# Attention inside a five-stage kernel: two score blocks in one PSUM bank, one reciprocal for four rows, Pool normalising every block, three copies for four, and q and k turned in the projections' banks

## What is computed

```python
x = x + quantised(layernorm(x)) @ quantised(ctx).T      # fp8 grid, blocks of 128
hidden = layernorm(x)
h = rmsnorm(hidden, attn_norm_w)
q, k, v = h @ q_w.T, h @ k_w.T, h @ v_w.T               # 16 heads of q, 4 of k and v, 128 columns each
q, k = rope(rmsnorm(q, q_norm_w)), rope(rmsnorm(k, k_norm_w))
scores = (q @ k.T) / sqrt(128)                          # causal
attn = softmax(scores) @ v                              # four q heads share one k and v head
hidden = hidden + attn @ o_w.T
moe = top-2 of 8 experts(rmsnorm(hidden, ffn_norm_w))
out = x + hidden + moe
```

## Time and profile before

| | |
|---|---|
| median of 3 runs | 1451.8 us (1449.87 to 1459.89) |
| the profiled execution | 1459.93 us, span of its instructions 1458.1 us |
| mean granted TensorE clock | 0.954 of full |
| first head's scores to the last head's values | 91 us to 1095 us, sixteen iterations |
| before it | the first sample's front and first projections |
| after it | last output projection, routing, experts (`moe`) |

### The profile page before, as it was taken

The page is one execution under the profiler, slowest core; times in us unless marked ns, Lnnn a source line. Parts: engine busy times, 40 slices in busy tenths (PEclk is TensorE's granted clock), DMA queues, the critical chain, the costliest instruction groups (busy, mean ns, idle before and its releaser), DMA issues. The chain is left out here.

```text
span 1458.1 us, 22564 instructions
## 1 busy us (share of the span) xinstructions
PE 1273.2 (87%) x6845; PEld 1025.1 (70%) x6845; DVE 837.7 (57%) x2459; ACT 719.7 (49%) x2289; POOL 382.8 (26%) x545
## 2 busy tenths in 40 slices
PE   1867899999999989789999999989994679999995
PEld 1555677787776778677767777778764569888995
DVE  7668877666876666568767666565535223222331
ACT  6447755556675655466655655556532123222331
POOL 0213222232322223032213133322210123333332
PEclk9988999999999999999999999999997689999998
DMA  2270425350535465547535565754214786774443
GB/s 95 82 265 22 147 110 176 131 196 9 221 100 205 147 217 194 180 134 209 182 134 192 178 208 177 211 193 158 87 59 174 273 290 188 206 222 79 82 74 44
DMA packets 89445, 227.85 MB, mean 156 GB/s; under 512 B 12081, under 2 KB 49841, under 8 KB 79089
## 3 DMA queue, kind: packets, MB, share of 16 engines
q1 hardware_dynamic: 75552, 201.21, 39.4%
q0 software_dynamic: 10848, 24.71, 9.3%
q10 hardware_dynamic: 2928, 0.49, 0.2%
HBM read 146.65 MB, written 79.72 MB: 155 GB/s over the span
## 5 line engine op out<-in xcount | busy, mean ns | idle before, releaser
L527 POOL TENSOR_TENSOR prob<-prob,rtotal 128x128 f32<-128x128 f32 (+2 forms) x192 | 116.7, 613 | 457.1 <-DVE rtotal L1270 430.6
L1264 DVE TENSOR_SCALAR_CACHE_REDUCE prob<-bank,nscale 128x128 f32<-128x128 f32 (+3 forms) x256 | 134.9, 544 | 164.9 <-PE bank L705 164.5
L944 ACT ACTIVATE prob<-prob,bias 128x128 f32<-128x128 f32 (+3 forms) x256 | 144.8, 566 | 153.1 <-DVE prob L1264 152.2
L669 PE MATMUL bank<-w_hi,hT_hi 128*128 128x512 f32 x480 | 175.3, 365 | 16.6 <-DVE rot L1229 16.6
L724 PE MATMUL bank<-pT,v 128*128 128x512 f32 (+3 forms) x512 | 175.8, 445 | 8.8 <-ACT pT L950 8.1
L950 ACT ACTIVATE pT<-bank 128x512 f32<-128x512 f32 (+3 forms) x256 | 103.8, 433 | 138.3 <-PE bank L713 137.9
L669 PE MATMUL bank<-w_hi,hT_lo 128*128 128x512 f32 x480 | 163.6, 341 | 0.0
L669 PE MATMUL bank<-w_lo,hT_hi 128*128 128x512 f32 x480 | 163.6, 341 | 0.0
L1529 PE MATMUL gu<-we,xT_hi 128*128 x624 | 155.9, 333 | 3.2 <-DVE xT_lo L1645 1.7
L504 POOL TENSOR_TENSOR r<-r,rot 128x640 f32<-128x640 f32 x60 | 100.2, 1670 | 189.8 <-DVE rot L1229 189.8
L703 PE MATMUL bank<-kT_hi,qT_hi 128*128 128x128 f32 (+3 forms) x256 | 103.5, 404 | 14.6 <-DVE prob L1264 14.5
(11 more groups left out here) (291 smaller groups left out, 2859.7 us busy)
## 6 DMA issues: line engine op xcount, KB each, us to landing
w_hi<-ws_scratch SPq DMA_DIRECT2D x24, 1024.0 KB, 5.2
w_lo<-ws_scratch SPq DMA_DIRECT2D x24, 1024.0 KB, 7.4
we<-wx_scratch SPq DMA_DIRECT2D x16, 1408.0 KB, 11.1
we<-wx_scratch SPq DMA_DIRECT2D x16, 768.0 KB, 9.2
stage<-in_wexp SPq DMA_DIRECT2D x64, 176.0 KB, 2.4
wx_scratch<-ehi SPq DMA_DIRECT2D x64, 176.0 KB, 2.6
wx_scratch<-stage SPq DMA_DIRECT2D x64, 176.0 KB, 2.7
stage<-in_wqkvo SPq DMA_DIRECT2D x40, 256.0 KB, 3.4
```

Of the source, the lines that this page charges most:

```text
L527: nc.gpsimd.tensor_tensor(p, p, rtotal[:, 4 * h + q:4 * h + q + 1].broadcast_to([P, KEYS[q]]), ALU.mult).then_inc(prob_ready, 1)
L669: last = nc.tensor.matmul(o, hT[a][:, k, t * P:(t + 1) * P], wkv(j, c, k) if kv else wq(j, c, k), start=(k == 0 and n == 0), stop=(k == KC ...
L944: nc.scalar.activation(p, p, ACT.Exp, bias=bias[:, 4 * h + q:4 * h + q + 1], scale=-1.0, accum_out=total[:, 4 * h + q:4 * h + q + 1]).then ...
L1264: nc.vector.tensor_scalar(prob[(G * it + h) % (LAG + 1)][:, P_AT[q]:P_AT[q] + KEYS[q]], bank[SC + q % 2][:, 0:KEYS[q]], nscale[it % 2][:, ...
```

## The change

Five edits, all in `mixer`, and one move in the table of the front.

- **Scores.** Blocks 0 and 1 of a head share one bank (columns 0 to 127 and 128 to 383) and one semaphore step; blocks 2 and 3 have a bank each. The three parts alternate between banks 3 and 4 across heads, and a part waits for the reading of the part two before.
- **Reciprocals.** DVE makes one reciprocal of a head's four row sums, a head later, after the next head's first two maxima. The multiplication on DVE is gone.
- **Normalising.** POOL multiplies all four blocks, in one go at the start of the next head.
- **Copies.** Key blocks 2 and 3 are turned into one bank and copied together: three copies for four. The three alternate between banks 5 and 6 across heads.
- **Turns.** q and k are turned in banks 0 and 1, in the order q0, k, q1, q2, q3. q0 stands in slot (3, 2) behind the last output tile; k, q1 and q2 in (3, 3); q3 in slot (0, 1) as before. `project` of the next iteration waits for all five low parts.
- **Front.** The maxima of the context are taken in four instructions in slots (0, 1) and (0, 2), POOL's reduction (`ca`) stands in (0, 3), the scales (`cs`) in (1, 1), and the scaling, rounding and scaling back of the first two tiles follow one to two slots later than before.

```diff
-        (3, 2): (('o', 3),),
-        (3, 3): (('t', 0), ('t', 1), ('t', 2), ('t', 3))}
+        (3, 2): (('o', 3), ('t', 1)),
+        (3, 3): (('t', 0), ('t', 2), ('t', 3))}
...
+PARTS = ((0, 1), (2,), (3,))
+TURNS = (1, 0, 2, 3, 4)
...
-        TR = (PT, PT + 1, AUX, PT, AUX)
+        SC_AT = (0, KEYS[0], 0, 0)
+        PT_COLS = (QS[0], QS[1], QS[2] + QS[3])
...
+        def score_bank(s, part):
+            return bank[SC + (3 * s + part) % 2]
+
+        def score_reads(fill):
+
+            return 4 * (fill // 3) + (2, 3, 4)[fill % 3] if fill >= 0 else 0
+
+        def pt_bank(s, m):
+            return bank[PT + (3 * s + m) % 2]
+
+        def turn_bank(i):
+            return bank[TURNS.index(i) % 2]
...
+            def normalise(s):
+                pool.wait_ge(inverted, s + 1)
+                for q in range(TT):
+                    p, n = prob[s % (LAG + 1)][:, P_AT[q]:P_AT[q] + KEYS[q]], 4 * (s % G) + q
+                    nc.gpsimd.tensor_tensor(p, p, rtotal[:, n:n + 1].broadcast_to([P, KEYS[q]]), ALU.mult).then_inc(prob_ready, 1)
...
                 if t == 0:
                     need(pe, o_added, TT * (j - 2))
+                    need(pe, qk_lo, (G + 1) * j)
...
+                turn = TURNS.index(i)
+                if turn == 0:
+                    pe.wait_ge(rope_added if j else first_added, TT * (j + 1))
+                    need(pe, o_added, TT * (j - 2) + 3 if j >= 2 else 0)
                 if i == 0:
                     pe.wait_ge(k_ready, j + 1)
-                    need(pe, pt_copied, 16 * it + 4 * (G - LAG))
+                    need(pe, o_added, TT * (j - 1) if j >= 2 else 0)
+                if turn >= 2:
+                    pe.wait_ge(qk_lo, (G + 1) * j + turn - 1)
...
+                need(pe, biased, score_reads(3 * s + part - 2))
+                for q in PARTS[part]:
+                    o = score_bank(s, part)[:, SC_AT[q]:SC_AT[q] + KEYS[q]]
...
+            def invert(s):
+                rows = slice(4 * (s % G), 4 * (s % G) + TT)
+                dve.wait_ge(exp_done, TT * (s + 1))
+                nc.vector.reciprocal(rtotal[:, rows], total[:, rows]).then_inc(inverted, 1)
```

The table of the front, one line of it:

```diff
-FRONT = ({(0, 1): (('cm', 0), ('cs', 0)),
+FRONT = ({(0, 1): (('cm', 0), ('cm', 1)),
```

167 lines of the change are left out of this document (66 added, 101 removed).

## The result

The changed kernel takes 1495.4 us (median of 4 runs, 1488.7 to 1495.9) against 1453.0 us for the kernel before (4 runs, 1449.9 to 1459.9): a ratio of 1.0258, 95% interval 1.0234 to 1.0282, which is 37 us. It is slower, as forecast, but by 37 us where the sum said 21. As a time, 1495.4 lies 3 us above the end of the range; as a ratio it lies inside (1492 over 1451.8 is 1.0277). The profiled execution took 1495.9 us, its span is 1494.1 us.

The account below looks back on a forecast made before the run. PE was taken to set the pace, busy 921.94 of 1004 us in the sixteen iterations. 26.2 + 8.5 - 12 + 4 - 7 + 1 = 20.7 on the 1451.8 us median gave 1472 us, 1.4% slower, range 1447 to 1492.

Parts of the forecast that it names:

- The wait in front of the projection: First projection of an iteration waits for DVE's low part of the fifth turn in bank 0: +26.2 us, at most 32.
- The clock behind it: PE's clock halves for 3.40 us behind five of fifteen new waits, 1.7 us each: +8.5 us.
- The context's maxima: Moved front gives POOL's reduction slots (0, 3) to (1, 1), so rotation waits less in three iterations: -12 us.
- best case of 20: Context's front: all 16.6 us of rotation waits go, plus 3.4 us, half of the half-clock time behind the longest.
- The turns: Iteration ends: q0's turn ahead of the last score block pushes the chain back 0.3 us, 14 times: +4, upper end 9.
- Scores, copies, reciprocals: Scores wait for DVE less often, parts waiting two back across heads: half of 14.5 us won, -7.
- POOL, +1: POOL's multiplications are hidden except in the last head, before PE: +1 us, between 0 and 2.8.
- the clock falling nearly everywhere: Rival: clock falls behind nearly every new wait, twelve more us, 1484 us; chance 0.12.
- The front going whole: Rival: front's stall in iterations 0, 4 and 8 goes whole and the clock holds, 1448 us; chance 0.23.
- The projection finding its turn done: Rival: PE reaches the projection late enough to find the turn done, 26.2 and 8.5 fall away, 1438 us; chance 0.07.
- POOL in DVE's way: Rival: POOL slows DVE's norm of k, delaying the iteration-end chain 0.7 us in 15 iterations, 1482 us; chance 0.06.
- the three that would have made the forecast wrong: New wait under 10 us; granted clock above 0.97; PE waiting for probabilities beyond the first heads of the three iterations.

Follow-up runs that it names:

- the scales later: Kernel with old turns and old front, plus scales and first rescaling two slots later, second rounding in head 1's second slot: 1439.7 us, ratio 0.9905.

## Why the prediction was right in its sign and about half in its size

A way from the old kernel to the new in steps that were each run (1% is 14.5 us): packed scores, reciprocals, copies and POOL, -11 us (0.9926); the turns into the projections' banks, all but the fifth, +11 (1.0004); the fifth turn there, with the wait, +20 (1.0139); the front, +17 (1.0258). Together 37. It is one way of several: since the parts don't add up, in another order each has another price (with the old turns the front costs 7, and the turns after it 41).

- *The wait in front of the projection, +26.2*: right. 28.0 us in 15 places, 1.4 to 2.3 each. Alone it measured 24.0. The reason that I gave, that DVE takes the low part after the maxima, fits seven places; in the other eight ACT's two copies end last, and most of those waits are 2.25 us where I had read 1.94, which only the upper end of 32 allowed for. What the sum did not have is that three of the waits fall on the same iterations as the rotation's stall, which gives back 8 us.
- *The clock behind it, +8.5*: right in kind, and near in size. I took five falls; four of the fifteen waits have one behind them, two where the wait was added alone. At 1.7 us each that is 6.8 us. PE's busy time grew by 11.6 us in all, so some falls stand behind other waits, which the sum did not price.
- *The context's maxima, -12*: this step failed, and it is the main error. I took three fifths of a best case of 20, and that was too large by itself: half clock over 4.17 us of PE's work costs 2.1 us and not 3.4. The rotation's wait fell about as far as forecast (10.9 us), but only 3.6 of these are the move's; the rest is gone with the front at its old place too, under the projection's wait. Waits for copies grew by 18.0 us, of which 11.6 are the move's and 6.4 came with the packed scores and copies. Part of this was in the text as the worst case, the row of scales, scalings, exponential and third copy; the price of the worst case, +5, left out the second stall, the rounding that now runs beside POOL, and that the rotation's stall would have been half hidden under the new wait. Alone the move costs 2 to 8 us in three pairs of kernels (the 2 within the noise), beside the wait 17, and it brings 12 in none.
- *The turns, +4*: probably too small. 11 us, give or take 4, by the two kernels that differ in them without the fifth's wait (1.0004 against 0.9926); the upper end was 9. In their profiles all waits of turns come to 42.7 us against 36.0. PE stands 11.8 us for an output's addition, while 8.7 us for the front's low part are gone. I had argued that the addition ends before ACT is free for k. At the end of iteration 4 it does (415.74, ACT is free at 416.46), but k's turn stands between the two, and PE waits for the addition all the same. What the rest of the 11 us is, beyond the 6.7 of waits, is not shown.
- *Scores, copies, reciprocals, -7, and POOL, +1*: right, -6 forecast, -11 measured together. The scores' wait went whole, and a part came back at the copies (14.6 with the old front against 8.1). No run shows a cost of POOL's multiplications in themselves.
- *The rivals*: the clock falling nearly everywhere did not happen (4 of 15). The front going whole is refuted by the run with the old front. The projection finding its turn done is refuted by its row. POOL in DVE's way was right as a mechanism and wrong in its place: the norm of k has a median of 689 ns now and 686 before, while the rounding is what it caught.

Of the signs that I named, the new wait (28.0), rotation (5.7), the scores (none left), k (26.0) stood as written, and the falls nearly (four, with a third forecast); none of the three that would have made the forecast wrong came true. What I had not named, a growing wait for copies, was the sign that was needed.

## What to carry to other kernels

A stall that is moved is worth what is left at its new place: before counting it as gained, list what stands in order behind it on each engine there (here ACT's copies, DVE's maxima), and which engine runs beside it now. Two stalls in the same stretch hide one another, so single edits don't add up: price an edit in the company it will have. And before giving a bank to a second user, look whether the engine that frees it is behind or ahead of the next one at that point; 1.4 to 2.3 us behind, fifteen times, was the largest single loss of this change.

## What the chip showed that I had not expected

Two steps of one rounding lost as much beside POOL, one behind the other, as the one row before the change showed for a single step. The rounding's third step, by line (ns: least, median, most), in the kernel before and in the changed one:

```profile
L1101 DVE SCALAR_TENSOR_TENSOR cb<-xm,cb x16: 691/693/694, 28.9 to 650.8; 128x512 f32<-128x512 f32 x16
```

```profile
L1110 DVE SCALAR_TENSOR_TENSOR cb<-xm,cb x16: 691/693/1931, 29.0 to 677.7; 128x512 f32<-128x512 f32 x16
```

At most 694 ns became at most 1931 ns, where POOL's work stands beside it: 1.24 us more, where the earlier trace rows has 1.22 more for the second step. POOL's four multiplications took 3.95 us there, and 2.75 in the next head:

```profile
667.97 2.75 POOL L545 TENSOR_TENSOR prob<-prob,rtotal 128x128 f32<-128x128 f32 x4 [2.58 <-DVE rtotal L1273]
```

With the rounding a slot later they still took 3.80, so it is not that rounding that lengthened them. The Trainium skill ("SBUF — State Buffer", Who interferes with whom) says that POOL and a DVE instruction with two SBUF inputs or in a two-port mode hold a shared port exclusively; the trace agrees, with DVE's 1.66 and 1.93 us beside two POOL sums of 1.7 us each, and with 0.43 and 0.69 us once the steps were moved away.

POOL stands idle on both sides of the reduction at every place tried: 5.9 us ahead and 7.0 behind in the changed kernel, 9.0 and 7.1 with the scales later. The idle time ahead can pass while POOL waits for the maxima: with the scales later, in iteration 0, the reduction started 0.1 us behind their end (98.48 to 98.62). The idle time behind it was 6.7 to 8.0 us each time. The Trainium skill ("GPSIMD Engine Reference", section on how an instruction is dispatched) gives about 6 us for the first call to a freshly loaded kernel; the 7.0 behind the reduction, when POOL goes back to an ordinary multiplication, is above that, so the measurement decides; whether both are one and the same cost no run here shows.
